# A transformer block on one core: in each slot, masks and scores of two maxima chunks move ahead of two score chunks

## The reference, cut to what matters

```
h = x @ W1 + b1                                   # 512 x 384, q, k, v of 16 heads, 8 wide
w = q @ k^T / sqrt(8);  causal mask;  softmax     # 512 x 512 for each head
x = layernorm(x + (w @ v) @ Wp + bp)
xr, xk = mu * x + (1 - mu) * x_prev               # x_prev: the token before
out = sigmoid(xr @ Wr) * (relu(xk @ Wk)^2 @ Wv)
x = layernorm(x + out)
```

## Time and profile before

| | |
|---|---|
| median of 3 runs | 741.61 us (740.34 to 743.75) |
| the profiled execution | 742.71 us, its span 740.9 us |
| mean granted TensorE clock | 0.927 |
| PE busy | 612.0 us (83%) |
| DVE busy | 548.0 us (74%) |
| ACT busy | 471.3 us (64%) |
| POOL busy | 372.9 us (50%) |

### The profile page before, as it was taken

How to read it: one execution, slowest core, us unless ns; L and a number is a source line. 1 busy time by engine, 2 the same in 40 slices (tenths; PEclk the granted TensorE clock), 3 DMA queues, 4 the chain that set the end, 5 groups by cost and what they waited for, 6 DMA issues and landing times.

```text
span 740.9 us, 17669 instructions
## 1 busy us (share of the span) xinstructions
PE 612.0 (83%) x6727; PEld 275.8 (37%) x6727; DVE 548.0 (74%) x1642; ACT 471.3 (64%) x916; POOL 372.9 (50%) x519
## 2 busy tenths in 40 slices
PE   3468887898989998998989898989989898978643
PEld 1132333343443434343434344343434353433232
DVE  1476785879797888888797979788888979772231
ACT  2104774777768676867677776867676767677510
POOL 3101343455646465565655555646555565555622
PEclk9555998999999999999999999999999999999855
DMA  4652525242525345353524252543535353100100
GB/s 146 104 130 46 144 46 158 46 144 49 144 45 141 78 86 134 60 158 60 158 57 144 49 146 46 127 92 75 143 61 158 60 140 57 25 18 17 30 14 15
DMA packets 72188, 65.80 MB, mean 89 GB/s; under 512 B 9318, under 2 KB 63911, under 8 KB 72103
## 3 DMA queue, kind: packets, MB, share of 16 engines
q1 hardware_dynamic: 71394, 64.41, 36.7%
q10 hardware_dynamic: 708, 0.26, 0.2%
HBM read 34.70 MB, written 29.88 MB: 87 GB/s over the span
## 4 chain that ended last, share of the span: by engine, by line
PE 58%; DVE 20%; ACT 8%; issue 6%; POOL 3%; DMA 3%; ACTq 1%; SPq 0%; POOLq 0%; DVEq 0%
PE ops L583 15%; DVE rowmax L750 12%; PE sps L556 10%; PE tps L518 9%; PE spare L444 8%; ACT probs L680 6%; PE spare L462 5%; PE sps L541 3%; DVE h L801 3%; PE spare L494 2%; PE spare L478 2%; DVE y L789 1%; PE spare L491 1%; PE spare L483 1%; PE spare L457 1%
## 5 line engine op out<-in xcount | busy, mean ns | idle before, releaser
L750 DVE TENSOR_REDUCE rowmax<-sps 128x1 f32<-128x512 f32 (+7 forms) x1024 | 401.2, 448 | 98.5 <-PE sps L556 97.9
L680 ACT ACTIVATE probs<-tps 128x512 f32<-128x512 f32 x640 | 346.3, 595 | 145.8 <-PE tps L518 145.7
L853 POOL TENSOR_SCALAR_AFFINE_SELECT probs<-probs 128x512 f32<-128x512 f32 x256 | 159.4, 641 | 256.9 <-ACT probs L680 256.7
L583 PE MATMUL ops<-probs,vop 128*32 128x384 f32 (+3 forms) x2048 | 172.7, 444 | 6.7 <-POOL probs L853 5.4
L518 PE MATMUL tps<-qop,kop 50*128 50x384 bf16 (+3 forms) x1024 | 126.6, 305 | 40.1 <-ACT probs L680 36.2
L556 PE MATMUL sps<-kop,qop 48*64 48x512 bf16 (+7 forms) x2048 | 130.4, 310 | 8.3 <-DMA kop<-d_parts 8.3
L541 PE MATMUL sps<-qmask,dup 64*128 64x128 bf16 (+1 forms) x640 | 69.7, 214 | 33.4 <-DVE rowmax L750 29.2
L518 PEld LDWEIGHTS tps<-qop,kop 50*128 50x128 bf16 x1024 | 34.2, 94 | 161.6 <-ACT probs L680 115.2
L583 PEld LDWEIGHTS ops<-probs,vop 128*32 128x32 f32 x2048 | 50.4, 109 | 80.4 <-issue 60.5
L556 PEld LDWEIGHTS sps<-kop,qop 48*64 48x64 bf16 x2048 | 43.1, 106 | 50.5 <-issue 19.3
L541 PEld LDWEIGHTS sps<-qmask,dup 64*128 64x128 bf16 x640 | 31.4, 95 | 75.8 <-DVE rowmax L750 69.5
(11 more groups left out here) (72 smaller groups left out, 581.3 us busy)
## 6 DMA issues: line engine op xcount, KB each, us to landing
qop<-d_parts SPq DMA_DIRECT2D x64, 192.0 KB, 4.3
kop<-d_parts SPq DMA_DIRECT2D x63, 192.0 KB, 4.7
d_parts<-qk_parts SPq DMA_DIRECT2D x15, 768.0 KB, 3.6
d_parts<-qk_parts SPq DMA_DIRECT2D x15, 512.0 KB, 4.9
d_parts<-qk_parts SPq DMA_DIRECT2D x17, 256.0 KB, 5.1
xa<-L_attn_x SPq DMA_DIRECT2D x16, 256.0 KB, 3.0
xres<-L_attn_x SPq DMA_DIRECT2D x16, 256.0 KB, 3.3
out<-result SPq DMA_DIRECT2D x16, 256.0 KB, 2.7
```

What stands on the lines that cost most here:

```text
L583: last = nc.tensor.matmul(ops[32 * t:32 * t + 32, BLK * a:SEQ], vop[:, par, a, QUARTET * half + t, hh, :], probs[:, g % 2, i, off:off + w] ...
L680: nc.scalar.activation(probs[:, g % 2, i, :], tps[:, bank(n), :], ACT.Exp, scale=SCALE)\
L750: last = nc.vector.reduce_max(rowmax[:, par, QUARTET * half + i, a:a + 1], sps[:, bank(n), off:off + w], axis=AX_X)
L853: last = nc.gpsimd.affine_select(out=v, in_=v, compare_op=ALU.is_ge, fill=0.0, base=0, pattern=[[0, QUARTET], [1, BLK]], channel_multiplie ...
```

## The change

In each place the call for T moves from ahead of M and S to behind them. Before, TensorE's order in a place was T, M, S, spare use; now it is M, S, T, spare use. `pv` stands after place 1 as before. No instruction is added or taken away, and the order of the instructions on ScalarE, VectorE, GpSimd and SyncE is the same.

```
                     for i in range(0, QUARTET, 2):
-                        if active("T", tb):
-                            t_chunks(before("T", tb), tg, i)
                         if active("S", b):
                             s_masks(before("S", b), g, i)
                             s_chunks(before("S", b), g, i)
+                        if active("T", tb):
+                            t_chunks(before("T", tb), tg, i)
                         for _, use, n in ORDER[b, g, i // 2]:
                             spare_use(use, n)
```

## The result

The changed kernel took 752.70 us (median of 4 runs, 749.90 to 754.44) against 741.84 us (740.34 to 743.75): a ratio of 1.0142, 95% interval 1.0103 to 1.0181. It is slower by 10.9 us. 756 was forecast, with 746 to 762 as the range. The profiled execution took 749.9 us, its span 748.1 us, clock 0.933.

A forecast was written before the change was run, and what follows sets the result against it. PE's stream was taken to set the pace. Per step -0.04 + 0.66 + 0.33 = 0.95 us, 13.3 over 14 steps, plus 1.0 for step 0: 14.3 us, giving 756 us, range 746 to 762.

The forecast's parts named there:

- The seams: PE's stream: 16 places a step each lose 0.10 us to changes of matmul shape, 1.6 us, partly hidden in waits.
- The turn-around of ACT: Slot 8: T now stands directly ahead of hT, so sums0 waits for ACT's copy and comes 0.69 us later.
- From sums0 to slot 4: Slot 8 to the next step's slot 4: 9 seams make 0.9 us, waits absorb 0.57, 0.33 remains.
- the walk: Following PE, ACT and DVE from slot 4 with timeline durations in the new order; gave 0.95 us a step.
- Slots 4 to 8: Seven seams there cost nothing by M of slot 8, which comes 0.04 us earlier.
- the edges: Outside the 14 full steps: 1.0 us for ten seams ahead of pv in step 0; step 15 unchanged.
- The room in the waits: PE's waits of T for ACT and M for DVE: 4.1 us a step in which added time can vanish.
- The smaller loss: Rival: seams vanish in PE's waits, only ACT's delay at hT in slot 8 counts; 748 us, chance 0.18.
- The rotation: Rival: same ring of matmuls, waits absorb all added time; 742 us, no change, chance 0.07.
- the larger loss: Rival: later exponentials delay GpSimd's zeroing and pv, 0.5 us more in each of 14 steps; 763 us, chance 0.08.
- The third, DVE as pace-maker: Rival: DVE paces slots 6 to 8, reductions begin sooner, 0.5 us a step gained; 735 us, chance 0.05.
- The step of 41.1 us: Sign in the profile: a middle step should last 41.1 us at unchanged clock; 40.2 or less would favour rivals.

The follow-up runs named there:

- e5: Kernel before, old order, with each mask matmul cut into two of 64 x 64; 735.33 us, ratio 0.9889.
- e4: Changed kernel with each mask matmul cut into two of 64 x 64; 733.41 us, ratio 0.9891.
- e2: Kernel before with only the two places of slot 8 in the new order; 755.40 us, ratio 1.0177.
- e6: Kernel before with both places of slots 1, 2 and 3 in the new order; 745.66 us, ratio 1.0062.
- e3: Kernel before with only place 1 of slot 7 in the new order; 741.64 us, ratio 0.9981 (interval takes in 1).
- e7: Changed kernel with mask matmuls cut into 64 x 64 and slot 8 back in the old order; 728.76 us, ratio 0.9822.
- e9: Kernel before with GpSimd's xbias block, which waits for a DMA, moved behind the zeroing of slot 3; 736.77 us, ratio 0.9906.

## Why the prediction was right

**The seams.** Right in mechanism and size. PE's busy time in a step grew by 1.5 us for a forecast of 1.6; S to T, T to G and G to M came out as read from the rows. e5, and the comparison of e4 with it, show that it is the change of shape that costs. The rule of the Trainium skill (TensorEngine Tiling (Array Packing), Key Properties), that a change of mode drains TensorE, agrees with e4 and e5, which give it a price of 0.08 to 0.1 us each time. What passes inside TensorE is not settled: a weight load that does not come ahead of its matmul is seen at the same seams, and the runs don't part the two.

**The turn-around of ACT.** Right, and the largest term: 0.65 us late at sums0 was forecast against M of slot 8. Measured in the changed kernel it is 2.61 - 1.93 = 0.68 us, by e2 0.69 us of the step. The row of step 15, where S is absent, showed it beforehand: from T to sums0 it took 2.11 us, and now 2.10 in a middle step (337.81 to 339.91).

**From sums0 to slot 4.** Forecast 0.33 us. In the traces pv of slot 7 comes 19.39 us before and 19.70 us after behind the start of slot 4 (339.14 - 319.75; 340.50 - 320.80), so 0.31 late, and the step ends 0.64 late: 0.33 us. e6 agrees, with 0.34 us for slots 1 to 3. But the walk had the wait of T for ACT in slot 0 shrink and not go, and all but about 0.1 us of it went (T at 305.48); over the whole step T's listed waits for ACT are none, where they were 2.0 us.

**Slots 4 to 8.** Here the sum was off: -0.04 us forecast, -0.37 measured (M of slot 8 at 336.62 - 319.75 = 16.87 before and 337.30 - 320.80 = 16.50 after). I had taken h at its 1.43 us. That duration was no property of the instruction; it held a collision with GpSimd's zeroing, which the later T moved away (e3). That is the whole difference between 0.95 and 0.64 us a step, 4.5 us of the total.

**The total.** 10.9 us were measured for 14.3 forecast. By the cuts at slot 4 the steps from there on cost 1.08 us, twelve times about 0.63, 1.03 and 0.46, and 1.56 lie ahead of them: the first T now stands behind M and S that wait for a reduction (61.16 in place of 59.64 us), and 0.20 us of it was there before (M at 59.31 in place of 59.11). I had 1.0 for all that lies outside the 14 steps; the edges were too small, and the step too large by 0.31. That the two misses go against each other, and bring the total nearer, is luck. So is a slip in the sum: it takes 0.66 us for the turn-around, where the working gives 0.69 ahead of the -0.04; with that a step is 0.98 and the whole 14.7 us.

**The room in the waits.** Read wrongly. The 29.2 us of M's waits hold 12.4 us ahead of the first T. In the 16 steps with T there were (36.2 + 16.8) / 16 = 3.3 us a step, and not 4.1. The longest of them was also not the one in slot 8 (0.78 us) but T's for ACT in slot 0 (0.92). The sum didn't rest on either, since it came from the walk through the slots.

**The rivals.** The smaller loss (748) had all seams vanish in waits; they did not (e6), and the step came out below the forecast for another reason, the shorter h. The rotation and the larger loss are out. The third, DVE as pace-maker, was judged wrongly: I wrote that DVE had no idle time to give in slots 7 and 8. e5 shows that it had 0.2 us in this one run. The new order didn't win it: its run of reductions takes 4.24 us, with S behind M as before. And the 2.1 us a step that this rival hoped to win from M's waits were 16.8 / 14 = 1.2 us, less than the seams it set against them.

**What was to be seen in the profile.** Right: S to T (0.35 us), T to G (0.32 us), the wait for the copy of hT (0.29 us), the exponentials 1.7 us later against DVE. The step of 41.1 us was 40.80. Wrong: the waits of M for DVE did not fall or stay, they rose to 52.0 us, and in the steps with T from 16.8 to 39.1. With T out of the way M reaches its wait earlier, and the wait says nothing of a loss.

## What to carry to other kernels

When two pieces of work change places in an engine's stream, count the seams between unlike shapes anew, and ask for each piece what shade it stood in: here T lost the shade of a wait, and ACT's answer came too late for the next use of one bank. A duration in a profile can hold a collision with another engine; before it goes into a sum, compare it with the same instruction elsewhere in the trace. A row of merged instructions without idle time is not proof of a full engine: compare its length with that of the same row in a kernel where the engine is fed sooner. A total of waits over the whole trace can hold stretches on which the change doesn't act: ask for the window. And before two profiled executions are subtracted, compare where each had the lower clock.

## What the runs showed of the hardware

T to M took 0.23 us with both in 64 rows x 128 columns (before) and 0.32 us with M in 64 x 64 (e5), for the same T; M to S took 0.16 us with unlike shapes (changed kernel) and 0.08 us with like ones (e4), though it then held four matmuls in place of two. Here, cutting a matmul in two to match its neighbour's shape made the seam cheaper.

Four DVE instructions of 128 x 128 took 1.11 us with no zeroing beside them (e3) and 1.43 us when a GpSimd zeroing of 128 x 512 lay beside the last of them, which ended 0.07 us behind it (before). In slot 9 of the changed kernel such a four took 1.35 us beside step_d. The exclusive hold on the port pair that DVE and GpSimd share, as the Trainium skill has it (SBUF — State Buffer, Who interferes with whom), would look like this; no run here separates it from other causes. Not every GpSimd instruction does it: beside rstd (128 x 4, 1.04 us), which lay over three of the four in the changed kernel, h took its 1.11 us.

In e3 the granted clock was 0.50 from 612.3 to 615.7 us and 1.00 around it, and pv took 1.94 us in it and 1.07 outside. Such stretches lie in seven of the twelve traces between 100 and 660 us (before, e2, e3, e4, e5, e7, e9), not always at the same place. In e3 the step took 1.2 us more, in e9 one took 2.15 us more. Executions that differ in them differ in time with one and the same kernel.
